# Compressed interaction network on one core: c and q chunks in blocks for unit 0, then in pairs; the stores of D split over two queues; SP waits for all gathers ahead of unit 1's x tiles

## The chip, the core and the metric

One core of a Trainium2 chip runs the whole program. The metric is the device time of one launch in microseconds (us), lower is better. The kernel before takes 185.9 us (median of 3 runs, 185.22 to 186.16).

## The reference

The input x has 512 samples, 40 features and 16 embedding columns d. Three layers are chained; each forms all products of a feature of x with a feature of the layer before and contracts them with a weight:

```python
for Wk, bk in zip(Ws, bs):
    z = jnp.einsum('bid,bjd->bdij', base, curr)
    curr = jnp.einsum('bdij,ijh->bhd', z, Wk) + bk[None, :, None]
    logit.append(curr)
pooled = jnp.sum(jnp.concatenate(logit, axis=1), axis=-1)
out = pooled @ lin_w + lin_b
```

W0 is 40 x 40 x 100, W1 and W2 are 40 x 100 x 100. Only the sum over d and the product with lin_w are wanted of the second and third layer, so the kernel folds W2 with lin_w into small vectors v, and v with W1 into one matrix D over pairs of features. What is left per sample and d is: c1 = (x x) times W0, q = (x x) times D (both 101 rows, the extra one carries the biases), and the sum of c1 * q over rows and d.

## The kernel before, in words

**The products.** A column of work is one sample and one d. 16 d times 512 samples are cut into U = 8 units of N = 1024 columns. The symmetric pairs of 41 features (the 41st is a constant one) are laid on K = 126 partitions in C = 7 chunks per unit, so there are NCH = 56 chunks, numbered m; unit 0 is m = 0 to 6, unit 1 is m = 7 to 13. The product tile of chunk m is formed by VectorE (`form`, L246), rounded by ScalarE to fp32r (`round_high`, L324, z_high) and its rest is taken by VectorE (`split`, L253, z_low). z_high and z_low have SLOTS = 14 places. In unit 0 the second factor comes from six small selection matmuls (`select_xb`, L476), later from a load of the tile xb_z (`load_xb`, L171) beside one x tile per unit (`load_xa`, L168), both by SP's DMA queue.

**The matmuls.** `chunk_products` (L434) is 6 matmuls: (high weight, high z), (low weight, high z), (high weight, low z), each for two halves of 512 columns. It is called by `c1_chunk` with W0's weights wc and by `q_chunk` with D's weights wq. The trace writes buffers without numbers: c_ps is the bank of c1, q_ps that of q. c1 of a unit is copied out by ScalarE (`copy_c1`, L331), q times c1 is added up by VectorE (`product`, L261 and L263). TensorE runs c1 LAG = 8 chunks ahead of q: c1 of m = 0 to 7 alone, then q(m), c1(m + 8) in turn, then the last eight q alone. The last two q chunks are done half by half (`last_q`, L443), and a short tail of VectorE, TensorE and ScalarE ends the program.

**The weights of q.** v comes from 40 small matmuls over W2 (`v_piece`, L495), a turn (L504) and a copy (`v_sb`, L356). D is made in NG = 5 groups (`d_group`, L518 and L521): each holds 5 lower features on partitions 0 to 63 and 5 upper ones on 64 to 127; group 4 holds the last lower feature alone. Two PSUM halves alternate, ScalarE copies each to SBUF (`copy_d`, L338, tile w_d), and a store (`store_d`, L159) writes it to d_dram: six stores on SP's queue, one on POOL's. When all have landed, 12 gathers (`gather_d`, L153) read it back in another layout into pair_sb. A gather has a side (0: contiguous rows of 808 or 2020 bytes; 1: rows of 404 bytes), one of T = 3 thirds of the partitions, and a piece: piece 0 is for chunks 0 and 1, piece 1 for chunks 2 to 6. ScalarE issues side 1 of piece 0, SP the other nine. Then the two sides are added, rounded and split: for chunks 0 and 1 by VectorE (`first_weights`, L279 to L284), for chunks 2 and 3 and then 4 to 6 by POOL (L419, L422, L424).

**The order.** All is written by hand, one stream per engine, with semaphores between. SP's stream is: x tile and first xb tile, W0's first part, small constants, the rest of W0, W2 (4 loads), W1 (4 loads), then unit 1's x tile (L195), unit 1's xb tiles for chunks 0 and 1, the stores, xb 2, three gathers, xb 3, six gathers, xb 4 to 6.

## Time and profile before

| | us |
|---|---|
| median of 3 runs | 185.9 (185.22 to 186.16) |
| profiled execution, its own time | 186.29 |
| its span, first to last instruction | 184.5 |
| TensorE busy in the span | 175.8 (95%) |
| VectorE busy | 151.8 (82%) |
| ScalarE busy | 73.9 (40%) |
| POOL busy | 16.2 (9%) |

The span is what the views show; launch and end around it are the other 1.8 us. All times in the rows count from the start of the span. A row of the timeline gives start, duration, engine, line, operation, tile written and tiles read, how many instructions were merged, and in brackets the idle time before it and what ended it. Consecutive matmuls overlap in the rows, so the distance between starts is what one costs, not its duration. Granted clock is 1.000 over the whole span.

### The profile page before, as it was taken

Reading aid. Unit: us, or ns where it says so; the run is one execution under the profiler, and the core shown is the slowest. Engines: PE = TensorE matmul, PEld = TensorE weight load, DVE = VectorE, ACT = ScalarE, POOL = GpSimd, SP = SyncE. Lnnn points to the kernel's source line nnn. Section 1 sums busy time; section 2 is a strip of 40 time slices with the busy share of each in tenths; the row PEclk is TensorE's granted clock in tenths of the full one; section 3 lists DMA queues with packets and bytes.
Section 4 is the critical chain, followed back from the end, with each engine's and each line's share of the span. In section 5 each row is a group of like instructions: output and inputs, shape, how many; then the busy total and the mean of one; then the engine's idle time right before and its main releaser. Section 6 shows DMA issues by size and latency. Waiting matters only on the chain.

```text
span 184.5 us, 2573 instructions
## 1 busy us (share of the span) xinstructions
PE 175.8 (95%) x814; PEld 118.7 (64%) x814; DVE 151.8 (82%) x135; ACT 73.9 (40%) x79; POOL 16.2 (9%) x21
## 2 busy tenths in 40 slices
PE   7798998869999999999999999999999999999994
PEld 2364474546677777777777777777777777777760
DVE  0699698869999999999999999999999999300622
ACT  2554664124444624462446244534453445002001
POOL 3670010087000000000000000000000000000000
PEclk9999999999999999999999999999999999999999
DMA  6999997999797739774986597659765200000000
GB/s 192 379 409 411 412 219 218 231 406 397 230 324 233 234 122 321 247 227 124 331 230 228 126 322 235 223 135 329 228 219 128 99 0 0 0 0 4 0 0 0
DMA packets 11845, 37.71 MB, mean 204 GB/s; under 512 B 2305, under 2 KB 2941, under 8 KB 11838
## 3 DMA queue, kind: packets, MB, share of 16 engines
q1 hardware_dynamic: 11538, 37.38, 62.1%
q0 software_dynamic: 48, 0.16, 0.3%
q10 hardware_dynamic: 252, 0.09, 0.3%
q8 instruction: 4, 0.07, 0.2%
q14 instruction: 3, 0.02, 0.0%
HBM read 36.28 MB, written 1.33 MB: 204 GB/s over the span
## 4 chain that ended last, share of the span: by engine, by line
PE 79%; DMA 8%; SPq 3%; POOL 3%; issue 2%; DVE 1%; ACT 1%; DVEq 0%; ACTq 0%
PE q_ps L434 39%; PE c_ps L434 36%; DMA pair_sb<-d_dram 3%; DMA pair_sb<-w_pairs 3%; DMA d_dram<-w_d 2%; PE q_ps L518 2%; SPq L153 2%; POOL pair_sb L401 1%; POOL wq_low L424 1%; PE q_ps L443 1%; POOL wc_low L406 1%; DVE xb_z L246 1%; ACT z_high L324 1%; SPq L159 1%; PE c_ps L565 1%
## 5 line engine op out<-in xcount | busy, mean ns | idle before, releaser
L324 ACT ACTIVATE z_high<-xb_z 126x1024 fp32r<-126x1024 f32 x56 | 59.2, 1060 | 73.0 <-DVE xb_z L246 69.3
L253 DVE TENSOR_TENSOR z_low<-xb_z,z_high 126x1024 fp32r<-126x1024 f32 x56 | 68.9, 1232 | 1.1 <-ACT z_high L324 0.8
L246 DVE TENSOR_TENSOR xb_z<-x_a,xb_z 126x1024 f32<-126x1024 f32 x50 | 62.1, 1242 | 8.3 <-DMA xb_z<-xw 8.3
L434 PE MATMUL q_ps<-z_high,wq_high 126*101 126x512 f32 x108 | 34.1, 396 | 3.0 <-POOL wq_low L424 1.5
L434 PE MATMUL c_ps<-z_high,wc_high 126*101 126x512 f32 x112 | 35.5, 398 | 0.2 <-issue 0.2
L434 PE MATMUL c_ps<-z_high,wc_low 126*101 126x512 f32 x112 | 35.0, 394 | 0.0
L434 PE MATMUL c_ps<-z_low,wc_high 126*101 126x512 f32 x112 | 35.0, 394 | 0.0
L434 PE MATMUL q_ps<-z_high,wq_low 126*101 126x512 f32 x108 | 33.8, 394 | 0.0
L434 PE MATMUL q_ps<-z_low,wq_high 126*101 126x512 f32 x108 | 33.7, 393 | 0.0
L434 PEld LDWEIGHTS q_ps<-z_high,wq_high 126*101 126x101 f32 x108 | 17.7, 165 | 10.8 <-POOL wq_low L424 2.0
L434 PEld LDWEIGHTS c_ps<-z_high,wc_high 126*101 126x101 f32 x112 | 18.0, 165 | 9.0 <-issue 1.6
L434 PEld LDWEIGHTS c_ps<-z_high,wc_low 126*101 126x101 f32 x112 | 18.5, 165 | 7.5
L434 PEld LDWEIGHTS c_ps<-z_low,wc_high 126*101 126x101 f32 x112 | 18.5, 165 | 7.4
L434 PEld LDWEIGHTS q_ps<-z_high,wq_low 126*101 126x101 f32 x108 | 17.9, 166 | 7.3
L434 PEld LDWEIGHTS q_ps<-z_low,wq_high 126*101 126x101 f32 x108 | 17.8, 165 | 7.2
L261 DVE TENSOR_TENSOR w_post<-q_ps,w_post 101x1024 f32<-101x1024 f32 x7 | 8.5, 1216 | 12.0 <-PE q_ps L434 12.0
L331 ACT ACTIVATE w_post<-c_ps 101x1024 f32<-101x1024 f32 x8 | 8.1, 1010 | 14.1 <-PE c_ps L434 14.1
L263 DVE TENSOR_TENSOR acc<-acc,w_post 101x1024 f32<-101x1024 f32 x7 | 8.6, 1226 | 0.2
L485 PE MATMUL q_ps<-warm_sb 128*128 128x512 bf16 x20 | 6.2, 483 | 1.4 <-POOL warm_sb L393 1.4
L267 DVE TENSOR_TENSOR w_post<-q_ps,w_post 101x256 f32<-101x256 f32 (+1 forms) x3 | 1.4, 508 | 5.2 <-PE q_ps L443 5.2
L388 ACT ACTIVATE out_sb<-c_ps,const_sb 1x512 f32<-1x512 f32 x1 | 0.7, 678 | 12.2 <-PE c_ps L568 12.2
L485 PEld LDWEIGHTS q_ps<-warm_sb 128*128 128x128 bf16 x20 | 2.3, 121 | 4.7 <-issue 2.2
(56 smaller groups left out, 66.1 us busy)
## 6 DMA issues: line engine op xcount, KB each, us to landing
xb_z<-xw SPq DMA_DIRECT2D x50, 512.0 KB, 4.5
x_a<-xa SPq DMA_DIRECT2D x8, 512.0 KB, 5.0
w_d<-w2h SPq DMA_DIRECT2D x4, 512.0 KB, 7.4
w_post<-w1x SPq DMA_DIRECT2D x3, 512.0 KB, 10.0
...
```

What stands on the lines that cost most here:

```text
L153: eng.dma_start(q_sides[P * t:P * (t + 1), side, c0 * J:c1 * J].rearrange("p (c j) -> p c j", j=J), src).then_inc(dpair_loaded[piece], 16)
L159: eng.dma_start(d_dram[r0:r1, column * J:(column + n) * J], w2_d[DR * upper + r0:DR * upper + r1, first * J:(first + n) * J]).then_inc(sto ...
L246: nc.vector.tensor_tensor(xb_z[0:K, c, :], x_a[0:K, u % 2, :], x_b, ALU.mult).then_inc(z_done, 1)
L253: nc.vector.tensor_tensor(z_low[0:K, m % SLOTS, :], xb_z[0:K, c, :], z_high[0:K, m % SLOTS, :].bitcast(fp32), ALU.subtract).then_inc(low_d ...
L261: nc.vector.tensor_tensor(prod, q_ps[u % 2][0:J, :], c1_sb[u % 2], ALU.mult).then_inc(q_psum_free, 1)
L263: nc.vector.tensor_tensor(acc[:, :], acc[:, :], prod, ALU.add).then_inc(acc_done, 1)
L324: nc.scalar.activation(z_high[0:K, m % SLOTS, :], xb_z[0:K, m % C, :], ACT.Copy).then_inc(high_done, 1)
L331: nc.scalar.activation(c1_sb[u % 2], c1_ps[u % 2][0:J, :], ACT.Copy).then_inc(c1_copied, 1)
L401: nc.gpsimd.tensor_tensor(side[:, :, 0, :], side[:, :, 0, :], side[:, :, 1, :], ALU.add).then_inc(wc_sums, 1)
L434: last = nc.tensor.matmul(ps[0:J, h * B:(h + 1) * B], w[0:K, c * J:(c + 1) * J], z[0:K, slot, h * B:(h + 1) * B], start=(c == 0 and k == 0 ...
L485: nc.tensor.matmul(warm_ps, warm_sb[:, 0:128], warm_sb[:, :], start=True, stop=True)
L518: last = nc.tensor.matmul(d_ps[g % 2][0:DR, 0:n], v_sb[:, :], w1_post[0:J, first:first + n], start=True, stop=True)
```

## The change

Seven things are changed.

1. **TensorE's order** (LAG is gone). After the D groups: c1 of m = 1 to 6, then q of m = 0 to 6, then c1(m), q(m) in turn, and c1(54), c1(55) ahead of the last q.
2. **The D groups** run in the order 4, 0, 1, 2, 3, with W1's loads in that order; c1(1) no longer stands between them. VectorE copies groups 1 and 3 (`copy_d` in its own stream), ScalarE 4, 0 and 2.
3. **Upper features** are placed by UPPER_AT, so that the group of features 31 to 35 and 36 to 40 is stored first, and the wrapped columns at the left of d_dram come from groups 0, 1 and 2.
4. **Stores**: seven on SP's queue, three on ScalarE's (upper half), none on POOL's; DS = 10 of them are awaited.
5. **Gathers**: SP issues all of side 0, ScalarE all of side 1.
6. **Unit 1's tiles**: SP waits until both pieces of the gathers have landed, then loads the x tile and the seven xb tiles of unit 1. W0's last part (chunks 3 to 6) is loaded after W1; its rounding on ScalarE stands after the stores.
7. **Weights of q**: VectorE prepares chunks 0 and 1 and chunks 2 and 3, POOL only 4 to 6. The product of unit u stands at m = 16 + 7u in VectorE's stream instead of 20 + 7u, the copy of c1 at 13 + 7u in ScalarE's instead of 16 + 7u.

```diff
-LAG = 8
 BODY = 2 * C
-PRODUCT_AT = 20
-C1_AT = 3 * C - LAG
+PRODUCT_AT = 16
+C1_AT = 2 * C - 1
...
-W1_CUTS = (0, 1, 2, 3, NG)
+W1_CUTS = (0, 1, 2, 3, 4, NG)
+W1_ORDER = (4, 0, 1, 2, 3)
+D_ORDER = (4, 0, 1, 2, 3)
+UPPER_AT = (31, 36, 26, 21)
...
-DS = 6
+DS = 10
...
-PREP_AT = 9
-GATHER_AT = 8
+GATHER_AT = 7
...
-            for i in range(1, len(WC_CUTS) - 1):
-                load_w0(i)
+            load_w0(1)
             for i in range(VP):
                 load_w2(i)
-            for i in range(len(W1_CUTS) - 1):
+            for i in W1_ORDER:
                 load_w1(i)
-            load_xa(1, 1)
-            for c in range(2):
-                sp.wait_ge(low_done, c + 1)
-                load_xb(1, c)
+            load_w0(2)
+            sp.wait_ge(dgroup_copied, 1)
+            store_d(sp, 0, LEFT + 4 * GI, 4 * GI, LOWER - 4 * GI, (0, DR))
             sp.wait_ge(dgroup_copied, 2)
-            store_d(sp, 0, LEFT, 0, 2 * GI, d_stored)
-            store_d(sp, 1, LEFT + LOWER, 0, 2 * GI, d_stored)
-            store_d(sp, 0, LEFT + F, 0, RIGHT, d_stored, (32, DR))
-            sp.wait_ge(dgroup_copied, 4)
-            store_d(sp, 0, LEFT + 2 * GI, 2 * GI, 2 * GI, d_stored)
-            store_d(sp, 1, LEFT + LOWER + 2 * GI, 2 * GI, 2 * GI, d_stored)
-            sp.wait_ge(dgroup_copied, NG)
-            store_d(sp, 0, LEFT + 4 * GI, 4 * GI, LOWER - 4 * GI, d_stored)
-            sp.wait_ge(low_done, 3)
-            load_xb(1, 2)
+            sp.wait_ge(dgroup_copied_dve, 1)
+            store_d(sp, 0, LEFT, 0, 2 * GI, (0, DR))
+            store_d(sp, 0, LEFT + F, 0, RIGHT, (32, DR))
+            sp.wait_ge(dgroup_copied, 3)
+            store_d(sp, 0, LEFT + 2 * GI, 2 * GI, GI, (0, DR))
+            store_d(sp, 1, LEFT - 2 * GI, 0, 2 * GI, (0, 32))
+            store_d(sp, 1, 0, 3 * GI - (LEFT - 2 * GI), LEFT - 2 * GI, (0, 32))
+            sp.wait_ge(dgroup_copied_dve, 2)
+            store_d(sp, 0, LEFT + 3 * GI, 3 * GI, GI, (0, DR))
             sp.wait_ge(equals_cleared, 1)
             sp.wait_ge(d_stored, 16 * DS)
-            sp.wait_ge(d_stored_pool, 16)
             for side, t, piece in GATHER:
-                if piece == 1 and (side, t) == (0, 0):
-                    sp.wait_ge(low_done, 4)
-                    load_xb(1, 3)
-                if side == 0 or piece > 0:
+                if side == 0:
                     gather_d(sp, side, t, piece)
-            for c in range(4, C):
+            for piece in range(len(WQ_CUTS) - 1):
+                sp.wait_ge(dpair_loaded[piece], 16 * sum(g[2] == piece for g in GATHER))
+            load_xa(1, 1)
+            for c in range(C):
                 sp.wait_ge(low_done, c + 1)
                 load_xb(1, c)
...
+            def copy_d(g):
+                dve.wait_ge(dgroup_done, D_ORDER.index(g) + 1)
+                nc.vector.tensor_copy(w2_d[:, g * GI * J:(g + 1) * GI * J], d_ps[0]).then_inc(dgroup_copied_dve, 1)
...
                 for m in range(m0, m0 + BODY):
+                    if m == 5:
+                        copy_d(1)
+                    if m == C:
+                        split(it, C - 1)
+                        first_weights(0)
+                        first_weights(1)
                     form(it, m)
+                    if m == 5:
+                        copy_d(3)
                     if m == 0:
                         split_x()
                         split(it, 0)
                     if m >= PRODUCT_AT and (m - PRODUCT_AT) % C == 0:
                         product(it, (m - PRODUCT_AT) // C)
-                    if m == PREP_AT:
-                        first_weights()
-                    if m > 1:
+                    if m > 1 and m != C:
...
+            copy_d(4)
             copy_d(0)
-            copy_d(1)
             round_high(0, 4)
             copy_d(2)
-            copy_d(3)
-            copy_d(4)
-            act.wait_ge(dgroup_copied, NG)
+            act.wait_ge(dgroup_copied, 3)
+            act.wait_ge(dgroup_copied_dve, 1)
+            store_d(act, 1, LEFT + UPPER_AT[0], 0, 2 * GI, (0, DR))
+            store_d(act, 1, LEFT + UPPER_AT[2], 2 * GI, GI, (0, DR))
+            act.wait_ge(dgroup_copied_dve, 2)
+            store_d(act, 1, LEFT + UPPER_AT[3], 3 * GI, GI, (0, DR))
+            cast_w0(2)
+            act.wait_ge(dgroup_copied, 3)
+            act.wait_ge(dgroup_copied_dve, 2)
             for m in range(5, BODY):
                 if m == GATHER_AT:
                     act.wait_ge(equals_cleared, 1)
                     act.wait_ge(d_stored, 16 * DS)
-                    act.wait_ge(d_stored_pool, 16)
-                    for t in range(T):
-                        gather_d(act, 1, t, 0)
+                    for side, t, piece in GATHER:
+                        if side == 1:
+                            gather_d(act, side, t, piece)
...
+            sum_w0(0)
+            sum_w0(1)
+            low_w0(0)
+            low_w0(1)
+            sum_w0(2)
+            low_w0(2)
             pool.wait_ge(wc_ready, len(WC_CUTS) - 1)
             nc.gpsimd.memset(q_sides[0:P, 1, 0:J], 0.0).then_inc(equals_cleared, 1)
             pool.wait_ge(equals_cleared, 1)
-            pool.wait_ge(dgroup_copied, 4)
-            store_d(pool, 1, 0, UPPER - LEFT, LEFT, d_stored_pool, (0, 32))
-            for i in range(1, len(PREP_CUTS) - 1):
-                cols = slice(PREP_CUTS[i] * J, PREP_CUTS[i + 1] * J)
-                if PREP_CUTS[i] in WQ_CUTS:
-                    piece = WQ_CUTS.index(PREP_CUTS[i])
-                    pool.wait_ge(dpair_loaded[piece], 16 * sum(g[2] == piece for g in GATHER))
-                    pool.wait_ge(wq_ready, 1)
-                nc.gpsimd.tensor_tensor(q_sides[0:K, 0, cols], q_sides[0:K, 0, cols], q_sides[0:K, 1, cols],
-                                        ALU.add).then_inc(wq_sums, 1)
-                pool.wait_ge(wq_sums, i + 1)
-                nc.gpsimd.tensor_copy(wq_high[0:K, cols], q_sides[0:K, 0, cols]).then_inc(wq_highs, 1)
-                pool.wait_ge(wq_highs, i + 1)
-                nc.gpsimd.tensor_tensor(wq_low[0:K, cols], q_sides[0:K, 0, cols], wq_high[0:K, cols].bitcast(fp32),
-                                        ALU.subtract).then_inc(wq_ready, 1)
+            cols = slice(PREP_CUTS[2] * J, PREP_CUTS[3] * J)
+            pool.wait_ge(dpair_loaded[1], 16 * sum(g[2] == 1 for g in GATHER))
+            nc.gpsimd.tensor_tensor(q_sides[0:K, 0, cols], q_sides[0:K, 0, cols], q_sides[0:K, 1, cols],
+                                    ALU.add).then_inc(last_sums, 1)
+            pool.wait_ge(last_sums, 1)
+            nc.gpsimd.tensor_copy(wq_high[0:K, cols], q_sides[0:K, 0, cols]).then_inc(last_highs, 1)
+            pool.wait_ge(last_highs, 1)
+            nc.gpsimd.tensor_tensor(wq_low[0:K, cols], q_sides[0:K, 0, cols], wq_high[0:K, cols].bitcast(fp32),
+                                    ALU.subtract).then_inc(last_ready, 1)
...
+                place = D_ORDER.index(g)
+                d_bank = d_ps[place % 2]
+                if place == 0:
                     pe.wait_ge(v_copied, 1)
-                if g == 1:
+                if place == 1:
                     pe.wait_ge(const_copied, 1)
-                if g in W1_CUTS:
-                    pe.wait_ge(w1_loaded[W1_CUTS.index(g)], 16)
-                if g >= 2:
-                    pe.wait_ge(dgroup_copied, g - 1)
+                pe.wait_ge(w1_loaded[g], 16)
+                if place == 2:
+                    pe.wait_ge(dgroup_copied, 1)
+                if place == 3:
+                    pe.wait_ge(dgroup_copied, 2)
+                if place == 4:
+                    pe.wait_ge(dgroup_copied_dve, 1)
...
+            d_group(4)
             d_group(0)
             d_group(1)
-            c1_chunk(0, 1)
             d_group(2)
             d_group(3)
             select_xb(6)
-            d_group(4)
-            for m in range(2, LAG):
+            for m in range(1, C):
                 c1_chunk(0, m)
-            whole = (NCH - LAG) // BODY
-            with pe.Fori(0, whole) as it:
-                for m in range(LAG, LAG + BODY):
-                    q_chunk(it, m - LAG)
+            for m in range(C):
+                q_chunk(0, m)
+            for m in range(C, BODY):
+                c1_chunk(0, m)
+                q_chunk(0, m)
+            with pe.Fori(0, NCH // BODY - 2) as it:
+                for m in range(BODY, 2 * BODY):
                     c1_chunk(it, m)
-            for m in range(LAG + whole * BODY, NCH):
-                q_chunk(0, m - LAG)
+                    q_chunk(it, m)
+            for m in range(NCH - BODY, NCH - 2):
                 c1_chunk(0, m)
-            for m in range(NCH - LAG, NCH - 2):
                 q_chunk(0, m)
+            for m in range(NCH - 2, NCH):
+                c1_chunk(0, m)
...
-        groups = [np.arange(g * GI, min((g + 1) * GI, LOWER)), np.arange(LOWER + g * GI, min(LOWER + (g + 1) * GI, F))]
-        part = w1f[:, np.concatenate(groups)].reshape(128, -1)
+        groups = [np.arange(g * GI, min((g + 1) * GI, LOWER)), np.arange(UPPER_AT[g], UPPER_AT[g] + GI) if g < NG - 1 else []]
+        part = w1f[:, np.concatenate(groups).astype(int)].reshape(128, -1)
```

SP's queue from W1's loads to unit 1's tiles. DMA names give the tile written and read; w0_pairs is W0, d_dram <- w2_d a store of D, pair_sb <- d_dram a gather. Before:

```order
L183 DMA w1_post<-w1x 128x1125
L168 DMA x_a<-xa 128x1024
L171 DMA xb_z<-xw 128x1024 [waits low_done] x2
L159 DMA d_dram<-w2_d 64x1010 [waits dgroup_copied]
...
L159 DMA d_dram<-w2_d 64x101 [waits dgroup_copied]
L171 DMA xb_z<-xw 128x1024 [waits low_done]
L153 DMA pair_sb<-d_dram 42x202 [waits d_stored_pool,d_stored,equals_cleared]
...
L171 DMA xb_z<-xw 128x1024 [waits low_done]
L153 DMA pair_sb<-d_dram 42x505
```

The same place of the changed kernel:

```order
L178 DMA pair_sb<-w0_pairs 128x808
L162 DMA d_dram<-w2_d 64x101 [waits dgroup_copied]
L162 DMA d_dram<-w2_d 64x1010 [waits dgroup_copied_dve,dgroup_copied]
L162 DMA d_dram<-w2_d 32x909
L162 DMA d_dram<-w2_d 64x505 [waits dgroup_copied]
L162 DMA d_dram<-w2_d 32x1010
L162 DMA d_dram<-w2_d 32x202
L162 DMA d_dram<-w2_d 64x505 [waits dgroup_copied_dve]
L156 DMA pair_sb<-d_dram 42x202 [waits d_stored,equals_cleared]
...
L156 DMA pair_sb<-d_dram 42x505 x3
L171 DMA x_a<-xa 128x1024 [waits dpair_loaded1,dpair_loaded0]
L174 DMA xb_z<-xw 128x1024 [waits low_done] x7
```

No x tile stands ahead of the stores or between the gathers any more; the first one stands behind a wait for both pieces.

VectorE's stream from the last selected product of unit 0 to unit 1's first products; xb_z is `form`, z_low is `split`, L279 to L284 are the weights of q. Before:

```order
L246 TENSOR_TENSOR xb_z<-x_a,q_ps0 126x1024 [waits selected,xa_loaded0]
L253 TENSOR_TENSOR z_low<-xb_z,z_high 126x1024 [waits z_slots_free,high_done]
L246 TENSOR_TENSOR xb_z<-x_a,xb_z 126x1024 [waits xb_loaded0,xa_loaded1]
...
L246 TENSOR_TENSOR xb_z<-x_a,xb_z 126x1024 [waits xb_loaded2,xa_loaded1]
L279 TENSOR_TENSOR pair_sb<-pair_sb 126x202 [waits dpair_loaded0]
```

The changed kernel, with the two copies of D ahead of it:

```order
L276 COPY w2_d<-q_ps1 128x505 [waits dgroup_done]
L245 TENSOR_TENSOR xb_z<-x_a,c1_ps1 126x1024 [waits selected,xa_loaded0]
L276 COPY w2_d<-q_ps1 128x505 [waits dgroup_done]
L252 TENSOR_TENSOR z_low<-xb_z,z_high 126x1024 [waits z_slots_free,high_done]
L245 TENSOR_TENSOR xb_z<-x_a,q_ps0 126x1024 [waits selected,xa_loaded0]
L252 TENSOR_TENSOR z_low<-xb_z,z_high 126x1024 [waits z_slots_free,high_done] x2
L282 TENSOR_TENSOR pair_sb<-pair_sb 126x202 [waits dpair_loaded0]
...
L282 TENSOR_TENSOR pair_sb<-pair_sb 126x202 [waits dpair_loaded1]
...
L245 TENSOR_TENSOR xb_z<-x_a,xb_z 126x1024 [waits xb_loaded0,xa_loaded1]
```

Unit 1's first product, which stood ahead of the first weights, stands behind both sets of weights.

ScalarE's stream from the rounding of z(3) to the gathers; w2_d <- q_ps1 is a copy of D. Before:

```order
L338 ACTIVATE w2_d<-q_ps1 64x101 [waits dgroup_done]
L324 ACTIVATE z_high<-xb_z 126x1024 [waits z_slots_free,z_done,dgroup_copied]
L324 ACTIVATE z_high<-xb_z 126x1024 [waits z_slots_free,z_done]
L324 ACTIVATE z_high<-xb_z 126x1024 [waits z_done,z_slots_free]
L153 DMA pair_sb<-d_dram 42x101 [waits d_stored_pool,d_stored,equals_cleared]
L153 DMA pair_sb<-d_dram 42x2x101 x2
```

The changed kernel:

```order
L347 ACTIVATE w2_d<-q_ps1 128x505 [waits dgroup_done]
L162 DMA d_dram<-w2_d 64x1010 [waits dgroup_copied_dve,dgroup_copied]
L162 DMA d_dram<-w2_d 64x505
L162 DMA d_dram<-w2_d 64x505 [waits dgroup_copied_dve]
L352 ACTIVATE wc_high<-pair_sb 126x404 [waits wc_sums]
L333 ACTIVATE z_high<-xb_z 126x1024 [waits z_done,z_slots_free,dgroup_copied_dve,dgroup_copied]
L333 ACTIVATE z_high<-xb_z 126x1024 [waits z_slots_free,z_done]
L156 DMA pair_sb<-d_dram 42x101 [waits d_stored,equals_cleared]
L156 DMA pair_sb<-d_dram 42x2x101 x2
L156 DMA pair_sb<-d_dram 42x5x101 x3
```

Three stores, the rounding of W0's last part and three more gathers have come into it.

## Rows read from the trace of the kernel before

**Rows 1.** Windows: stretch, length, busy time (instructions) of the engines, clock, DMA share, GB/s.
```profile
60.00:80.00 20.00, 20.00 (x88) 14.23 (x87) 19.96 (x19) 9.99 (x10) 0.00 (x0) 1.00 0.74 232
```

**Rows 2.** Timeline of TensorE.
```profile
16.43 0.64 PE L518 MATMUL q_ps<-w_post,v_sb 101*64 101x505 f32 x1 [0.37 <-ACT v_sb L356]
...
17.32 0.59 PE L518 MATMUL q_ps<-w_post,v_sb 101*64 101x505 f32 x1
...
21.65 0.73 PE L476 MATMUL q_ps<-z_high,select_r 126*128 126x512 f32 x2
...
22.63 0.70 PE L434 MATMUL c_ps<-z_high,wc_high 126*101 126x512 f32 x2
...
33.10 0.70 PE L434 MATMUL q_ps<-z_high,wq_high 126*101 126x512 f32 x2 [1.50 <-DVE wq_low L284]
...
40.44 0.71 PE L434 MATMUL q_ps<-z_high,wq_high 126*101 126x512 f32 x2 [1.50 <-POOL wq_low L424]
...
43.30 0.62 PE L434 MATMUL q_ps<-z_high,wq_high 126*101 126x512 f32 x2
```

**Rows 3.** Timeline of VectorE.
```profile
6.08 1.23 DVE L246 TENSOR_TENSOR xb_z<-x_a,xb_z 126x1024 f32<-126x1024 f32 x1 [6.08 <-DMA xb_z<-xw]
...
17.48 1.23 DVE L253 TENSOR_TENSOR z_low<-xb_z,z_high 126x1024 fp32r<-126x1024 f32 x1
...
31.88 0.37 DVE L279 TENSOR_TENSOR pair_sb<-pair_sb 126x202 f32<-126x202 f32 x1 [0.87 <-DMA pair_sb<-d_dram]
...
47.47 1.21 DVE L246 TENSOR_TENSOR xb_z<-x_a,xb_z 126x1024 f32<-126x1024 f32 x1
...
49.74 1.21 DVE L246 TENSOR_TENSOR xb_z<-x_a,xb_z 126x1024 f32<-126x1024 f32 x1
...
178.83 0.69 DVE L267 TENSOR_TENSOR w_post<-q_ps,w_post 101x512 f32<-101x512 f32 x1 [5.20 <-PE q_ps L443]
```

**Rows 4.** Chain of waits: start, length, what.
```profile
23.51 4.53 DMA d_dram<-w_d
...
31.58 0.41 SPq L153
...
32.04 5.49 DMA pair_sb<-d_dram
```

**Rows 5.** Timeline of ScalarE (ACTq is its DMA queue).
```profile
16.41 1.04 ACT L324 ACTIVATE z_high<-xb_z 126x1024 fp32r<-126x1024 f32 x1
17.54 0.59 ACT L338 ACTIVATE w_d<-q_ps 128x505 f32<-128x505 f32 x1
...
22.74 0.25 ACT L338 ACTIVATE w_d<-q_ps 64x101 f32<-64x101 f32 x1 [0.38 <-PE q_ps L518]
...
28.11 1.40 ACTq L153 DMA_DIRECT2D pair_sb<-d_dram  x3
```

**Rows 6.** Timeline of SP's queue.
```profile
0.76 0.41 SPq L168 DMA_DIRECT2D x_a<-xa  x1
...
19.01 5.15 SPq L159 DMA_DIRECT2D d_dram<-w_d  x6
```

**Rows 7.** Tile d_dram, all its stores.
```profile
DMA to landing us min/median/max: 3.5/4.4/4.8
```

**Rows 8.** Windows while the stores, then the gathers of piece 1 are under way.
```profile
22.00:23.00 1.00, 1.00 (x6) 0.50 (x5) 0.51 (x1) 0.61 (x2) 0.05 (x1) 1.00 1.03 409
23.00:28.00 5.00, 5.00 (x23) 3.58 (x22) 4.60 (x5) 3.07 (x3) 0.61 (x1) 1.00 0.92 232
...
34.00:36.00 2.00, 2.00 (x11) 1.36 (x10) 1.31 (x3) 0.00 (x0) 0.00 (x0) 1.00 1.15 203
```

**Rows 9.** Timeline of POOL.
```profile
37.61 0.61 POOL L419 TENSOR_TENSOR pair_sb<-pair_sb 126x202 f32<-126x202 f32 x1 [14.00 <-DMA pair_sb<-d_dram]
...
40.35 1.82 POOL L419 TENSOR_TENSOR pair_sb<-pair_sb 126x303 f32<-126x303 f32 x1
...
43.64 1.69 POOL L424 TENSOR_TENSOR wq_low<-pair_sb,wq_high 126x303 fp32r<-126x303 f32 x1
```

More of the change, by code:

```diff
@@ L154, in gather_d, with store_d @@
                          ).then_inc(dpair_loaded[piece], 16)
-        def store_d(eng, upper, column, first, n, stored, rows=(0, DR)):
+        def store_d(eng, upper, column, first, n, rows):
             r0, r1 = rows
             eng.dma_start(d_dram[r0:r1, column * J:(column + n) * J],
-                         w2_d[DR * upper + r0:DR * upper + r1, first * J:(first + n) * J]).then_inc(stored, 16)
+                         w2_d[DR * upper + r0:DR * upper + r1, first * J:(first + n) * J]).then_inc(d_stored, 16)
         def chunks(tile, c0, c1):
@@ L345, in _ @@
             nc.scalar.activation(select_r[:, :], select_sb, ACT.Copy).then_inc(select_rounded, 1)
-            for i in range(len(WC_CUTS) - 1):
-                act.wait_ge(wc_sums, i + 1)
-                nc.scalar.activation(chunks(wc_high, WC_CUTS[i], WC_CUTS[i + 1]),
-                                     w0_sides[0:K, WC_CUTS[i]:WC_CUTS[i + 1], 0, :], ACT.Copy).then_inc(wc_highs, 1)
+            cast_w0(0)
+            cast_w0(1)
             round_high(0, 1)
```

52 lines of the change are left out of this document (29 added, 23 removed).

## The prediction

> **What bounds the kernel now.** I read the windows of the steady stage first. TensorE and VectorE are both busy for all of it [rows 1], so the reader must ask which of them waits for the other. VectorE's starts tell: two instructions lie 2.27 us apart (47.47 to 49.74) [rows 3], so a chunk (form and split) costs 2.27 us and a unit 7 x 2.27 + 2.27 for its two product instructions = 18.2 us. TensorE needs 2.86 us for a pair of chunks (40.44 to 43.30) [rows 2], 2.79 us on the mean of the long stretch below. That is 19.5 us a unit. TensorE is the bound and VectorE catches up 1.3 us a unit.
>
> Then the timeline of TensorE, from the back. VectorE's last product starts at 178.83, released by the first half of the last q [rows 3]. Before it TensorE is never idle back to 40.44, where it had waited 1.50 us for POOL's weights, and it had waited 1.50 us at 33.10 for VectorE's [rows 2]. At 43.30 q(3) begins; by then c1 of m = 0 to 10 and q of 0 to 2 are done, 14 chunks. From there to the first half of the last q are 97 chunks (51 q, 45 c1, and two half chunks): (178.8 - 43.3) / 97 = 1.40 us each. The tail behind it is the same in both kernels. So the end is set by one number: when TensorE, having 14 chunks done, goes on without a gap. Before it is 43.30.
>
> The chain of waits says what made that late: the last store starts at 23.51 and lands 4.53 us later, at 28.04; the gathers follow, the last issued at 31.58 and landed at 37.53 [rows 4]; then POOL's three operations to 40.4 [rows 9].
>
> **The change: the mark to compute.** After the change 14 chunks are done when q(6) ends (c1 0 to 6, q 0 to 6), and c1(7) comes next. From there it is again 49 c1 + 47 q + 1 = 97 chunks. Call its start T; the time changes by T - 43.30. c1(7) needs TensorE free from q(6), and z(7), whose x tiles are now loaded behind all gathers. Two paths, worked out from S, the moment all stores have landed.
>
> **Copies and stores: S.** TensorE starts the first D group at 16.43 and a whole group takes 0.89 us (16.43 to 17.32) [rows 2]. Group 4 (a fifth of the columns of one half) is done by 16.7, group 0 by 17.5. ScalarE rounds z(3) until 17.45 [rows 5], then copies group 4 (0.25 us) and group 0 (0.59 us) until 18.3. Group 1 can start at 17.7 and is done at 18.7. VectorE's split(3) ends at 18.7 too [rows 3], so its copy of group 1 runs to 19.3. A VectorE copy of 505 columns from PSUM isn't in the trace; 0.59 us (ScalarE, same tile) and 0.69 us (VectorE, 512 columns, two inputs) [rows 3, 5] bound it, I take 0.6. Group 2 is done at 19.5 and copied by 20.2 behind the rounding of z(4); group 3 at 20.4, and VectorE has formed z(5) meanwhile, so its copy ends at 21.1. Before, the last copy ended at 22.99 [rows 5]. SP's seven stores: the first tiny one at 18.3, two at 19.4, three from 20.2, the last from about 22.1 (six issues took 5.15 us with their waits, so 0.5 to 0.6 each [rows 6]). ScalarE's three fall between 20.3 and 21.9. The last store starts 1.4 us earlier than 23.51. Landing takes 3.5 to 4.8 us [rows 7], measured while loads of x tiles were in the same queue; these are now gone, so I take 3.9 (between the least and the median of 4.4): S = 26.0 instead of 28.04. With 3.5 us and 4.8 us it is 25.6 and 26.9.
>
> What limits it from the other side is the rate. 1.33 MB are written, and while the stores were under way 232 GB/s flowed at a DMA share of 0.92 [rows 8], against 409 GB/s while loads and stores were mixed just before [rows 8]. If that rate also held here, the first large store would land at 19.4 + 3.5 = 22.9 and the other 1.07 MB need 4.6 us more: S = 27.5. If lower and upper half, now in two queues, go side by side at more than 232 GB/s, S is bounded by the last issue: 22.1 + 3.5 = 25.6, or 25.3 if its start is a little earlier.
>
> The Trainium skill speaks against the second queue: "DMA: Bandwidth & Descriptors", section Rules for kernel authors, says that two transfers to disjoint partition halves serialize and that spreading DMAs over SP and ScalarE only saves issue time. "SBUF — State Buffer", section Door 1, says that partitions 0 to 63 reach only half of the ports. The 232 GB/s agree with half of the ports for each store by itself; by the first page S stays at about 27.5, by the second one interleaving could lift the rate and give 25.3.
>
> **From S to q(0).** The third gather of piece 0 on ScalarE starts 1.0 us after the first (three took 1.40 us [rows 5]), piece 0 was there at 31.88, 3.8 us after 28.06 [rows 3], and TensorE started at 33.10. I keep that with a small discount for the x tile that no longer shares the engines: q(0) at S + 4.9 = 30.9. Is TensorE free? c1(1) starts after select(6), which now follows group 3: 20.4 + 0.7 = 21.1, against 22.63 for c1(2) before [rows 2]; six chunks of 1.40 us end at 29.5. W0's last part is cast on ScalarE behind the stores, at 22.4, and subtracted by POOL, 404 columns, until 23.5 to 24.5; c1(3) wants it at 23.9. So c1(6) ends between 29.5 and 30.1, and TensorE idles about 1 us instead of 1.50. All of ScalarE's six gathers are issued by S + 2.9, ahead of q(0), which waits for a signal behind them. q(0) to q(6) take 7 x 1.40 = 9.8 us: q(6) ends at S + 14.7.
>
> **Piece 1 and unit 1's tiles.** Six gathers on each queue, 0.47 us each: the last issue ends at S + 2.9. From the end of the last issue to VectorE's first weights piece 0 took 31.88 - 29.51 = 2.4 us [rows 3, 5]; piece 1 took 5.49 us [rows 4], with an xb tile ahead of it and three behind. I take 3.5, nearer to the lower because no xb tile is left: L = S + 6.4 = 32.4; the ends are S + 5.3 and S + 8.4. VectorE then needs 1.1 us for chunks 2 and 3: ready at S + 7.6, wanted for q(2) at S + 7.7. POOL's chunks 4 to 6 took 40.35 to 45.33 beside a busy VectorE [rows 9]; its sum over 202 columns, with VectorE idle, took 0.61 us, over 303 columns beside VectorE 1.82 us. VectorE is idle now for most of that time, so 3.6 us: S + 10.1, wanted at S + 10.5. If it took the 4.98 us, 1 us more of idle.
>
> SP issues the x tile at L + 0.1. In the prologue x tile and xb tile were issued from 0.76 on and VectorE started at 6.08 [rows 3, 6], 5.3 us; with the engines already warm and idle, I take 4.9 (4.3 to 5.3). form(7) at L + 5.0; form(8) waits for the next 0.5 MB, 1.3 us; then split(7): z(7) is complete 3.7 us after form(7) starts, T = L + 8.7 = 41.1. The TensorE path gives S + 14.7 = 40.7. The later one counts: T = 41.1, a gain of 2.2 us.
>
> **What the tiles' delay costs later.** form(7), which stood ahead of the first weights (31.88), moves to 37.4. From then on VectorE gains 2.79 - 2.27 = 0.52 us a chunk on TensorE and pays 2.27 us for each product, the first at m = 16: c1(15) finds z(15) 1.9 us early, c1(22) 3.3 us early. Seven xb tiles stand in the queue at once at 1.3 us each, faster than 2.27. So no new stall. At the end c1(55) now comes just ahead of the last q; its copy (1024 columns on ScalarE, as the 1.04 us of a rounding [rows 5]) lies beside the first half of last q (1.40 us). Nothing.
>
> **Sum.** The profiled execution took 186.29; 186.29 - 2.2 = 184.1. It is 0.4 above the median of 185.9, so I say 185.9 - 2.2 = 183.7 for the likeliest case.
>
> **Rivals.**
> - *The halves go side by side* (S = 25.3, L = S + 5.2 = 30.5). TensorE's path decides: T = 40.0 and gain 3.3, time 182.6. For it: the low rate of single stores at a nearly full share. Against: the gathers' own packets are slow, 203 GB/s at a share of 1.15 [rows 8]. Chance 0.18.
> - *The stores keep their rate* (S = 27.5, L = 33.9): T = 42.6, gain 0.7, time 185.2. For it: the rows of the store stage, and the Trainium skill's rule above. Then the second queue does not do what it is there for. Chance 0.19.
> - *Slower: unit 1's tiles become the bound.* Place: VectorE's form(7). Price: T = L + 8.7, and before no product waited for the gathers. The point is L = 34.6; later than that the kernel loses. Piece 1 took 9.5 us from S before (28.04 to 37.53). If it keeps that with S = 26.0, L = 35.5, T = 44.2: 0.9 us lost, 186.8. Against: an xb tile of 0.5 MB stood ahead of it and its nine gathers on SP were issued one after the other until 32.0 [rows 4]. Chance 0.10.
> - *The wait at q(0) grows* over 2 us, and TensorE's clock falls to 1.2 GHz, where a chunk would cost twice 1.40 us. The two waits of 1.50 us [rows 2] left a chunk at its 1.40 us and the clock at 1.00 [rows 8]. Chance 0.03, about 186.5.
>
> The likeliest case has 0.50, its own range is 182.9 to 184.7. What a measurement of this kernel can tell from no change is about 0.5%, 0.93 us. Faster than 184.97: nearly all of the likeliest, the first rival and a third of the second, 0.74. Within: 0.16. Slower than 186.8: 0.10. The range that should hold 8 in 10 is 182.3 to 186.2.
>
> **What would show it.** In the changed profile: the last store issued near 22.1 and landed near 26.0; q(0) at 30.9 after about 1 us of idle; no wait of TensorE within q(0) to q(6); form(7) at 37.4 after some 4 us in which VectorE waited for xb; c1(7) at 41.1, at most 0.5 us after q(6); from there no gap, and the same 135.5 us from c1(7) to the start of the last product. It is wrong if the stores land after 27, if piece 1 lands more than 7 us after them, if POOL's three operations hold up q(4), or if a later c1 waits for a split.

## The result, and the profile after the change

The changed kernel takes 183.63 us (median of 5 runs, 183.48 to 184.47) against 185.9 for the kernel before in the same comparison: ratio 0.9876, 95% interval 0.984 to 0.9913. Forecast were 183.7 us and "faster". The profiled execution is the slowest of the five, 184.47 with a span of 182.7; before it was 186.29, so the profile has 1.8 of the 2.3 us. Runs over 1.5% above the fastest of their kernel count as slow, and medians and ratios here leave them out (five of `e9`'s twelve, one of `e11`'s six).

The page of the changed kernel:

```profile
span 182.7 us, 2555 instructions
...
PE 175.1 (96%) x814; PEld 118.8 (65%) x814; DVE 152.8 (84%) x140; ACT 72.7 (40%) x77; POOL 9.8 (5%) x17
```

TensorE's timeline: its last wait at q(0), and c1(7), the mark of the prediction. These answer to [rows 2]:

```profile
31.95 0.71 PE L453 MATMUL q_ps<-z_high,wq_high 126*101 126x512 f32 x2 [1.39 <-DVE wq_low L287]
...
41.82 0.63 PE L453 MATMUL c_ps<-z_high,wc_high 126*101 126x512 f32 x2
```

VectorE's, answering to [rows 3] (the copies of D's groups 1 and 3, the weights of both pieces, form(7), the last product):

```profile
18.48 0.68 DVE L276 COPY w_d<-q_ps 128x505 f32<-128x505 f32 x1
...
21.00 0.68 DVE L276 COPY w_d<-q_ps 128x505 f32<-128x505 f32 x1 [0.72 <-PE q_ps L547]
...
30.82 0.37 DVE L282 TENSOR_TENSOR pair_sb<-pair_sb 126x202 f32<-126x202 f32 x1 [3.82 <-DMA pair_sb<-d_dram]
...
32.59 0.37 DVE L282 TENSOR_TENSOR pair_sb<-pair_sb 126x202 f32<-126x202 f32 x1 [0.70 <-DMA pair_sb<-d_dram]
...
37.55 2.54 DVE L245 TENSOR_TENSOR xb_z<-x_a,xb_z 126x1024 f32<-126x1024 f32 x2 [3.17 <-DMA xb_z<-xw]
...
177.02 0.69 DVE L266 TENSOR_TENSOR w_post<-q_ps,w_post 101x512 f32<-101x512 f32 x1 [9.85 <-PE q_ps L462]
```

The last product starts at 177.02 instead of 178.83: this is the whole difference. It is 135.2 us behind c1(7), against 135.5 behind the mark before, so 1.5 of the 1.8 us were gained by the mark and 0.3 behind it. What matters lies ahead of 41.82. There the stores land at 26.34 (28.04 before) by the chain of waits, which answers to [rows 4] (start, length, what):

```profile
22.17 0.89 SPq L162
23.06 0.04 issue
23.10 3.23 DMA d_dram<-w_d
...
27.46 3.33 DMA pair_sb<-d_dram
...
31.95 10.04 PE q_ps L453 x42
```

and piece 1 lands at 32.59 instead of 37.53, 6.25 us behind the stores instead of 9.5. POOL's share of the last weights, [rows 9] before, is done by 35.1:

```profile
32.71 0.94 POOL L438 TENSOR_TENSOR pair_sb<-pair_sb 126x303 f32<-126x303 f32 x1 [7.76 <-DMA pair_sb<-d_dram]
33.72 0.44 POOL L441 CAST wq_high<-pair_sb 126x303 fp32r<-126x303 f32 x1
34.23 0.84 POOL L443 TENSOR_TENSOR wq_low<-pair_sb,wq_high 126x303 fp32r<-126x303 f32 x1
```

### The profile page after: what moved, and what is told of

Same layout as the page of the kernel before. It is cut to its first block, busy times and chain, and to the rows that moved or that the text cites. A ratio compares the mean times of both kernels' runs of the same rounds, so it can differ in the third digit from the quotient of the medians.

```text
span 182.7 us, 2555 instructions
## 1 busy us (share of the span) xinstructions
PE 175.1 (96%) x814; PEld 118.8 (65%) x814; DVE 152.8 (84%) x140; ACT 72.7 (40%) x77; POOL 9.8 (5%) x17
## 3 DMA queue, kind: packets, MB, share of 16 engines
HBM read 36.28 MB, written 1.33 MB: 206 GB/s over the span
## 4 chain that ended last, share of the span: by engine, by line
PE 86%; DMA 6%; DVE 2%; SPq 2%; issue 1%; ACTq 1%; ACT 0%; DVEq 0%
PE q_ps L453 41%; PE c_ps L453 38%; DMA xb_z<-xw 2%; SPq L162 2%; DMA pair_sb<-d_dram 2%; DMA d_dram<-w_d 2%; PE q_ps L516 1%; PE c_ps L497 1%; PE q_ps L544 1%; PE q_ps L462 1%; DVE z_high L271 1%; PE q_ps L497 1%; PE c_ps L594 1%; ACTq L156 1%; PE c_ps L597 0%
## 5 line engine op out<-in xcount | busy, mean ns | idle before, releaser
L245 DVE TENSOR_TENSOR xb_z<-x_a,xb_z 126x1024 f32<-126x1024 f32 x50 | 60.9, 1218 | 9.6 <-DMA xb_z<-xw 9.5
L544 PE MATMUL q_ps<-w_post,v_sb 101*64 101x505 f32 (+1 forms) x10 | 4.4, 537 | 0.8 <-ACT v_sb L368 0.4
```

The source lines that it names most:

```text
L245: nc.vector.tensor_tensor(xb_z[0:K, c, :], x_a[0:K, u % 2, :], x_b, ALU.mult).then_inc(z_done, 1)
L544: last = nc.tensor.matmul(d_bank[0:DR, 0:n], v_sb[:, :], w1_post[0:J, first:first + n], start=True, stop=True)
```

## The experiments

The marks are those of the prediction: S all stores landed, L piece 1 landed. All ratios are to the kernel before, run beside each kernel. "A" and "B" are the theories of each quoted text.

Every run has its granted clock, averaged over its span, beside its time. Runs of one kernel fall into two groups by it: most have 0.998 to 1.000, some 0.991 and less. The kernel before is in the lower group in 18 of its 69 runs beside the experiments, with a median of 186.8 us against 185.7. `e12` shows such a fall in its trace. Where a kernel has both groups, both are given.

**The stores by themselves** (`e7_store_rates`). A kernel of stores alone. In four stages it writes lower halves on SP; lower and upper by turns on SP; lower on SP and upper on ScalarE; whole tiles of 128 partitions.

> Only stores, nothing of the function is computed. Four stages, each 2.07 MB, each after the one before has landed: (1) eight stores of 64 lower partitions x 1010 columns on SP; (2) eight on SP, lower and upper by turns; (3) four lower on SP and four upper on ScalarE at the same time; (4) four stores of 128 partitions on SP. Theory A (a store of 64 partitions alone is limited by its half of the ports): (1) near 220 GB/s, (2) and (3) above it, (4) near 400. Theory B (the rate is that of writing to memory, or halves serialize): all of (1) to (3) near 230 GB/s; then (4) tells the two apart, 230 or 400.

One window of each stage (the last three numbers are granted clock, DMA share, GB/s):

```profile
14.00:15.00 1.00, 0.00 (x0) 1.00 1.01 206
24.00:25.00 1.00, 0.00 (x0) 1.00 0.91 307
35.00:36.00 1.00, 0.00 (x0) 1.00 0.98 372
42.00:43.00 1.00, 0.00 (x0) 1.00 1.03 412
```

Apart from the windows in which a stage begins (202 in the second, 109 and 190 in the third) or ends, the stages had 194 to 210, 247 to 307, 299 to 372 and 396 to 416 GB/s. That is what A expected: halves do go side by side, also from one queue, more so from two. That two transfers to disjoint partition halves serialize, as the Trainium skill's "DMA: Bandwidth & Descriptors" has it in its section Rules for kernel authors, does not hold for these stores of 64 partitions to HBM. That partitions 0 to 63 reach half of the ports, as the Trainium skill's "SBUF — State Buffer" has it in its section Door 1, fits the first row, which has half the rate of the last.

**The D part alone** (`e9_stores_gathers_only`): the kernel before with the new order of D's groups and columns, the copies on two engines, W0's last part late, ten stores and split gathers. Unit 1's tiles, the weights and TensorE's order stay old. Its core:

```diff
+D_ORDER = (4, 0, 1, 2, 3)
-DS = 6
+DS = 10
...
-                if side == 0 or piece > 0:
+                if side == 0:
```

> The kernel before with only what is ahead of the weights changed: order of the D groups, copies on two engines, ten stores on two queues, side 1 of all gathers on ScalarE, W0's last part late. TensorE's order, the places of unit 1's tiles and the weights (VectorE chunks 0 and 1, POOL 2 to 6) are those of before. Theory A (the gain is earlier stores and gathers; the block order and the wait only suit each other): stores land near 27, piece 1 near 35 with tiles beside it, q(2) at about 37.3 instead of 40.44, both waits of 1.5 us gone or nearly, 182.9 us (182.4 to 184). Theory B (order and wait are needed): piece 1 at 37 or later, 185 us or more.

186.45 us, ratio 1.0014 (0.9973 to 1.0054): nothing gained, A is wrong. SP's queue, POOL's wait, TensorE's wait at q(2) and the clock there:

```profile
17.12 7.34 SPq L163 DMA_DIRECT2D d_dram<-w_d  x7
...
28.16 1.17 SPq L157 DMA_DIRECT2D pair_sb<-d_dram  x3
```

```profile
37.59 0.62 POOL L444 TENSOR_TENSOR pair_sb<-pair_sb 126x202 f32<-126x202 f32 x1 [12.95 <-DMA pair_sb<-d_dram]
```

```profile
41.17 0.70 PE L459 MATMUL q_ps<-z_high,wq_high 126*101 126x512 f32 x2 [2.49 <-POOL wq_low L449]
```

```profile
41.00:42.00 1.00, 0.83 (x4) 0.64 (x5) 1.00 (x1) 0.00 (x0) 1.00 (x2) 1.00 1.06 422
```

The stores leave nearly as early as in the changed kernel (17.12 + 7.34 = 24.5 against 24.07) and still land at 28.1; piece 1 lands 9.4 us later. Both are the numbers of the kernel before. The DMA engines still moved 372 to 412 GB/s from 20 to 25, loads and stores mixed, where the changed kernel's moved 157 to 271. After the wait of 2.49 us the clock stayed at 1.00.

**All but the D part** (`e12_old_d_part`): the kernel before, with the change's TensorE order, late tiles, weights on two engines and split gathers:

```diff
-PRODUCT_AT = 20
-C1_AT = 3 * C - LAG
+PRODUCT_AT = 16
+C1_AT = 2 * C - 1
-            load_xa(1, 1)
-            for c in range(2):
-                sp.wait_ge(low_done, c + 1)
-                load_xb(1, c)
...
+            for piece in range(len(WQ_CUTS) - 1):
+                sp.wait_ge(dpair_loaded[piece], 16 * sum(g[2] == piece for g in GATHER))
+            load_xa(1, 1)
```

> The changed kernel with the D part of before: groups 0 to 4 in order, all copies on ScalarE, six stores on SP and one on POOL, W0's last part early. Late tiles, split gathers, block order and weights stay as changed. Theory A (the tiles' new place, not the D part, moved the stores' landing): the last store is issued at 23.5 as before, with no tile in the queue it lands 3 to 3.5 us later, at 26.5 to 27.0 instead of 28.04; c1(7) starts at about 41.5, 183.6 to 184.4 us. Theory B (the D part carries the earlier landing): it lands at 28, c1(7) at 43, 185.3 us or more.

186.16 us, ratio 0.9988 (0.9953 to 1.0023): again nothing, the time that B named and not my A's. By the clock the twelve runs are four at full clock, 185.10 to 185.38 us, and eight at 0.991, 185.88 to 186.98. The profile is of the second kind. SP's queue, TensorE's wait and the windows behind it:

```profile
19.14 5.19 SPq L159 DMA_DIRECT2D d_dram<-w_d  x6
27.85 2.48 SPq L153 DMA_DIRECT2D pair_sb<-d_dram  x6
```

```profile
32.44 1.18 PE L427 MATMUL q_ps<-z_high,wq_high 126*101 126x512 f32 x2 [2.46 <-DVE wq_low L278]
```

```profile
32.00:33.00 1.00, 0.56 (x2) 0.43 (x3) 0.37 (x1) 0.00 (x0) 0.00 (x0) 0.57 0.69 137
33.00:34.00 1.00, 1.00 (x4) 0.72 (x3) 0.13 (x1) 0.00 (x0) 0.07 (x1) 0.50 0.00 0
...
36.00:37.00 1.00, 1.00 (x6) 0.71 (x5) 0.00 (x0) 0.00 (x0) 0.35 (x1) 1.00 1.00 401
```

The copies keep the last store until 23.69; it lands 4.09 us later, S = 27.8, though no tile stands in the queue. The gathers gain (L = S + 6.1), but TensorE now waits 2.46 us at q(0), its clock falls to 0.50 (1.2 GHz) towards the end of that wait, and it is at 1.00 again from 36 on. q(0) to q(6) take 11.2 us instead of 9.87 (from q(0) to c1(7): 32.44 to 43.66, and 31.95 to 41.82). So all but the D part is worth 0.5 to 0.7 us while the clock stays up (185.2 against 185.7 to 185.9 for the kernel before at full clock), and the fall takes that back in two runs of three. With the D part S comes 1.5 us earlier, and none of the changed kernel's five runs has the lower clock. Two variants of it, `e1` and `e5`, have it in four runs of twelve and three of nine.

**TensorE's order alone** (`e4_order_only`), put on the kernel before:

```diff
-PRODUCT_AT = 20
-C1_AT = 3 * C - LAG
+PRODUCT_AT = 16
+C1_AT = 2 * C - 1
-            for m in range(2, LAG):
+            for m in range(2, C):
```

> The kernel before with only TensorE's new order (c1 0 to 6, q 0 to 6, then c1(m), q(m) in turn; products at m = 16 + 7u, copies of c1 at 13 + 7u). Theory A (the order alone loses, since without the c1 chunks between them q(2) and q(4) wait for POOL's weights of 40.4 and 45.3): q(4) at 45.4, q(6) ends at 49.6, 14 chunks done 6.3 us later than 43.30, 192 us. Theory B (the order is what gains): 184 us.

191.79 us, ratio 1.0285 (1.0233 to 1.0337), as A had it. Two waits, and the clock behind them:

```profile
32.40 0.71 PE L434 MATMUL q_ps<-z_high,wq_high 126*101 126x512 f32 x2 [2.33 <-DVE wq_low L284]
...
40.03 1.18 PE L434 MATMUL q_ps<-z_high,wq_high 126*101 126x512 f32 x2 [3.05 <-POOL wq_low L424]
...
44.95 0.71 PE L434 MATMUL q_ps<-z_high,wq_high 126*101 126x512 f32 x2 [0.43 <-POOL wq_low L424]
```

```profile
34.00:35.00 1.00, 1.00 (x4) 0.60 (x3) 0.95 (x1) 0.00 (x0) 0.00 (x0) 0.50 1.26 232
...
42.00:43.00 1.00, 1.00 (x4) 0.72 (x3) 1.00 (x2) 0.14 (x1) 1.00 (x1) 0.50 1.03 410
```

**The old order in the changed kernel** (`e10_old_order`), the reverse of that edit:

> The changed kernel with TensorE's order of before (c1 0 to 7 alone, then q(m), c1(m + 8)), products and copies at their old places. Theory A (the late tiles need the block): c1(7) must wait for z(7) at 41.2, q(0) starts at 42.6 with 8 chunks done instead of 14, 9 us later than now, 192.8 us, more if the clock falls in the long wait (12 us idle). Theory B (the order is of little weight): under 187 us.

195.19 us, ratio 1.0495 (1.0446 to 1.0543), the direction of A and 2.4 us above its number. c1(7) stands ahead of the first q chunks and waits for the late tile:

```profile
41.45 1.15 PE L454 MATMUL c_ps<-z_high,wc_high 126*101 126x512 f32 x2 [11.12 <-ACT z_high L334]
```

Its clock falls to 0.50 within that wait and stays there until nearly 45. So the late tiles need the order of blocks (without it 11.6 us more than the changed kernel, the clock's part included), and the blocks need piece 1 of the weights early (6 us, `e4`).

**Tiles not held back** (`e2_tiles_unbound`):

```diff
-            for piece in range(len(WQ_CUTS) - 1):
-                sp.wait_ge(dpair_loaded[piece], 16 * sum(g[2] == piece for g in GATHER))
```

> The changed kernel without SP's wait for the gathers ahead of unit 1's x tiles; the tiles follow the last gather in SP's queue. Theory A (TensorE's path through q(0) binds, the tiles only just do not): z(7) is ready near 37 instead of 41.2, piece 1 lands at most 0.7 us later, c1(7) still follows q(6) at 41.8, 183.6 us, within 0.4. Theory B (the wait protects the gathers from 4 MB of tiles on the same engines): piece 1 lands 2 us or more later than 32.6, q(2) or q(4) waits for its weights, 185 us or more.

186.3 us, ratio 1.0056 (1.0015 to 1.0096): B, though piece 1 lands 1.8 us later than in the changed kernel and not 2. Taking the wait out loses the whole gain. By the clock the ten runs are six at full clock, median 186.0, and four at 0.991, near 188.0.

```profile
34.40 0.37 DVE L280 TENSOR_TENSOR pair_sb<-pair_sb 126x202 f32<-126x202 f32 x1 [2.71 <-DMA pair_sb<-d_dram]
```

```profile
36.22 0.71 PE L451 MATMUL q_ps<-z_high,wq_high 126*101 126x512 f32 x2 [1.44 <-DVE wq_low L285]
```

Piece 1 comes at S + 8.1 and q(2) waits. Until piece 1 landed the tiles flowed beside it, up to 348 GB/s in all from 33 to 34. That ScalarE's gathers were late because they shared the engines with them is argued from this; the next run bears on it.

**No wait, but all gathers of piece 1 in SP's queue ahead of the tiles** (`e11_piece1_one_queue`):

```diff
-                if side == 0:
+                if side == 0 or piece > 0:
...
-            for piece in range(len(WQ_CUTS) - 1):
-                sp.wait_ge(dpair_loaded[piece], 16 * sum(g[2] == piece for g in GATHER))
```

> As the kernel without the wait (tiles unbound, 186.3 us), but all six gathers of piece 1 stand on SP's queue ahead of the tiles; ScalarE issues only side 1 of piece 0. Theory A (the 404-byte packets on ScalarE's ring lost their turns to the 4096-byte packets of the tiles on SP's): in one ring they come first; piece 1 lands near 33, 184 us. Theory B (tiles hold up gathers in either ring): piece 1 at 34.4 or later, 186 us or more.

184.15 us, ratio 0.9898 (0.9853 to 0.9942): A. A sixth run took 218.5 us at a mean granted clock of 0.759; why the clock was low is open. SP's queue and VectorE:

```profile
26.13 3.79 SPq L156 DMA_DIRECT2D pair_sb<-d_dram  x9
29.97 0.40 SPq L171 DMA_DIRECT2D x_a<-xa  x1
```

```profile
32.44 0.37 DVE L280 TENSOR_TENSOR pair_sb<-pair_sb 126x202 f32<-126x202 f32 x1 [1.59 <-DMA pair_sb<-d_dram]
...
35.38 2.50 DVE L243 TENSOR_TENSOR xb_z<-x_a,xb_z 126x1024 f32<-126x1024 f32 x2 [1.16 <-DMA xb_z<-xw]
```

The tiles start 2.5 us before L here and do little harm: they are behind the gathers in one queue, not beside them in another. They also start 1.1 us later than in `e2` (29.97 against 28.86), and how much of the difference is that and how much the queue is not separated. Also form(7) comes 2.2 us earlier and the time doesn't fall: VectorE's tile did not set c1(7).

**One queue for the stores** (`e1_one_queue`): ScalarE's three stores are issued by SP.

> The changed kernel with all ten stores of D on SP's queue (ScalarE issues none). Theory A (the end of the stores is set by when the last one is issued): nine large stores from 19.25 at some 0.5 us each put the last issue at about 24.0 instead of 23.10, the stores land at 27.3 instead of 26.34, c1(7) starts 1 us later, 184.6 us. Theory B (the bytes set it, halves serialize): landing stays at 26.3, 183.6 us. Theory C (lower and upper half side by side from two queues raise the rate): landing 1.5 to 2 us later, 185.4 us.

184.29 us, ratio 0.9939 (0.9905 to 0.9972). The last store starts at 24.00 and lands 2.37 us later, S = 26.37, unchanged, as B had it; ten issues end at 24.6:

```profile
17.04 7.56 SPq L162 DMA_DIRECT2D d_dram<-w_d  x10
```

The runs fall in two groups, eight near 184.1 at full clock and four near 185.8 at 0.991. At full clock it is 0.5 us above the changed kernel, which is not settled.

**All copies of D on ScalarE** (`e5_copies_scalar`):

> The changed kernel with all five copies of D on ScalarE. Theory A (the copies on VectorE save one wait for the rounding of z): group 3 is copied at about 22 as now (it waits for W1's load until 19.9), the last store moves by under 0.4 us, 183.6 to 184.0 us. Theory B (two copying engines carried the earlier stores): last store 1 us later, 184.6 us.

184.23 us, 0.9926 (0.9892 to 0.996). It overlaps with the changed kernel's interval. The medians differ by 0.6 us, by 0.4 for the six runs at full clock: VectorE's part in the copies is worth little here. The last store on the way to S starts at 22.06, 1.04 us earlier than in the changed kernel, and lands 4.47 us later, S = 26.55.

**Chunks 2 and 3 of the weights on POOL instead of VectorE** (`e3_pool_weights`):

> The changed kernel with the weights of chunks 2 and 3 prepared by POOL again, ahead of 4 to 6; VectorE only prepares chunks 0 and 1. Theory A (POOL is quick while VectorE waits): chunks 2 and 3 ready at about 34.4, wanted at 34.8; 4 to 6 ready at 36.8, wanted at 37.6; nothing moves, 183.6 us. Theory B (moving them to VectorE carried part of the gain): they take the 2.8 us of before, q(2) starts 0.6 us late and q(4) up to 2 us late, 184.2 to 186 us.

183.84 us, 0.9886 (0.9855 to 0.9917): A, no difference. POOL has chunks 2 and 3 ready at 33.92, 1.74 us after it began; q(2) starts at 33.97, under 0.2 us late. In the changed kernel VectorE takes 1.79 us for them (32.59 to 34.38), with POOL at work beside it: its cast takes 0.79 us instead of the 0.27 alone, its subtraction 0.56 instead of 0.37.

**Unit 1's x tile and first xb tile ahead of the stores** (`e8_tile_early`):

```diff
+            load_xa(1, 1)
+            sp.wait_ge(low_done, 1)
+            load_xb(1, 0)
```

> The changed kernel with unit 1's x tile and its first xb tile loaded ahead of the stores, behind W0's last part. Theory A: 1 MB more in the queue from 18 to 20.5, when the engines were nearly idle; the stores land up to 1 us later and the whole is 0 to 1 us slower than the changed kernel, since z(7) did not bind. Theory B (VectorE's wait for the tiles binds): c1(7) earlier, 183 us or less.

184.0 us, 0.9896 (0.9857 to 0.9936): A. S = 26.31; two tiles of 0.5 MB ahead of the stores do no harm and no good. They flow from 18 to 21 (397, 418 and 322 GB/s), before most bytes of the stores. `e9` has a third tile ahead of the stores and one right behind them, and there S is 28.1.

**A block of eight** (`e6_block_of_eight`): on top of that edit, c1(7) stands in the block ahead of q(0), where TensorE waits.

```diff
-            for m in range(1, C):
+            for m in range(1, C + 1):
...
-                c1_chunk(0, m)
+                if m > C:
+                    c1_chunk(0, m)
```

> As the kernel with the early tile, and c1(7) in TensorE's block ahead of q(0), where TensorE waits 1.4 us in the changed kernel. Theory A: one chunk more is done when q(6) ends, so 1.4 us are gained, less what the stores land later (0 to 1 us): 182.2 to 183.2 us, unless z(8), whose xb tile now comes first behind the gathers, is late at q(7). Theory B (what lands later eats it): 183.6 us or more.

VectorE's first weights and ScalarE's gathers move one chunk later with it. 182.51 us (182.34 to 182.87), ratio 0.9812 (0.9775 to 0.9849): A, faster than both kernels, each of its six runs below each of the changed kernel's, and 1.5 us below `e8`, from which it differs by the block alone. Without idling TensorE goes from c1(7) to q(0):

```profile
30.99 0.63 PE L455 MATMUL c_ps<-z_low,wc_high 126*101 126x512 f32 x2
31.46 0.62 PE L455 MATMUL q_ps<-z_high,wq_high 126*101 126x512 f32 x2
```

## Why the prediction was right

The size was right, forecast 183.7, measured 183.63, and so was the mechanism from S on. How S comes about was not: the number of that step is luck. Step by step, in the profiled execution:

| step | forecast | measured |
|---|---|---|
| last store issued | 22.1 | 23.10 |
| its landing | 3.9 | 3.23 |
| S | 26.0 | 26.34 |
| TensorE's idle at q(0) | about 1 | 1.39 |
| q(0) | S + 4.9 = 30.9 | S + 5.6 = 31.95 |
| q(0) to c1(7) | 9.8 | 9.87 |
| L | 32.4 | 32.59 |
| form(7) | 37.4 | 37.55 |
| c1(7) | 41.1 | 41.82 |
| c1(7) to the last product | 135.5 | 135.2 |

*S.* I took the issue of the last store plus a landing time, and was right by two errors that cancel. SP issued its stores more slowly while ScalarE issued at the same time: up to 1.15 us for one, where I took 0.5 to 0.6 (alone, in `e1`, up to 0.95). In return the last landed faster than the row of before. But S does not follow the last issue at all:

| | last store starts | lands after | S |
|---|---|---|---|
| `e5` | 22.06 | 4.47 | 26.55 |
| changed kernel | 23.10 | 3.23 | 26.34 |
| `e1`, one queue | 24.00 | 2.37 | 26.37 |

The starts are those of the issue; counted from its end (23.79, 24.07, 24.60) the landing shrinks as well. What the three have in common is the flow of bytes, here for the changed kernel, `e1` and `e5`:

```profile
20.00:26.00 6.00, 5.63 (x24) 3.29 (x25) 4.69 (x6) 2.71 (x4) 2.06 (x3) 1.00 0.84 220
...
20.00:26.00 6.00, 6.00 (x28) 4.29 (x27) 5.38 (x6) 2.56 (x3) 2.34 (x3) 1.00 0.83 218
...
20.00:26.00 6.00, 4.60 (x20) 2.70 (x17) 3.10 (x3) 3.23 (x5) 2.57 (x3) 1.00 0.91 218
```

That is the 1.33 MB of the stores, from 20 on. My other reason, that no x tile is in the queue, holds for the amount and not for the tile as such: with two tiles ahead S is 26.3 (`e8`), with three ahead and one behind 28.1 (`e9`), where loads still fill the engines. Without tiles but with the old D part S is 27.8 (`e12`), with a window of 77 GB/s at 23 while the late copies hold up the stores. So S wants the first large store out early, no gap behind it, and the loads done by then. This is read from the windows; no run changed the amount of bytes. Why the flow has 220 GB/s here and 299 to 372 in `e7`'s third stage stays open.

*The rate of the stores* (second rival, 0.19). Single windows of the changed kernel reach more than the 232 GB/s of [rows 8] (clock, share, GB/s last):

```profile
22.00:23.00 1.00, 1.00 (x6) 0.73 (x5) 1.00 (x2) 0.00 (x0) 0.00 (x0) 1.00 0.99 271
...
24.00:25.00 1.00, 0.63 (x3) 0.23 (x2) 0.41 (x2) 1.00 (x2) 0.89 (x2) 1.00 0.97 259
```

On the mean of 21 to 26 it is 232 again. So the rival's rate held and its sum was wrong: it let the bytes begin with the landing of the first large store at 22.9, and they flow from 20 on. The first rival's premise, halves side by side, holds (`e7`), yet S did not come at 25.3; `e5`, with its last issue at 22.06, did not reach it either. One queue gives the same S (`e1`), so the second queue is not where S came from. That interleaving two stores could lift the rate was my own inference from the ports, not a statement of the Trainium skill.

*q(0)* is the mis-sized term, by 0.7 us. In this execution piece 0 came at S + 4.5. In those of `e1`, `e8` and `e11`, whose stores landed at 26.37, 26.31 and 26.1, q(0) started at 30.78, 31.07 and 30.90, on my 30.9, and c1(7) at 41.07, 41.06 and 41.30, near my 41.1. They are kernels of 181.9 to 182.2 us of span, and the changed kernel's other executions had 181.7 to 181.9, against 182.7 in the profiled one. I take the profiled one as late by this, which is argued from these numbers and not shown.

*T.* I let VectorE's path decide (41.1) over TensorE's (40.7). z(7) was complete at 41.2, as said. TensorE's path ended 0.6 us behind that, at 41.8 instead of 40.7, because of q(0). `e11` agrees: with form(7) at 35.4 the time is no lower. The 0.4 between my two paths was less than the error of either.

*The weights of chunks 2 to 6.* I gave VectorE 1.1 us for chunks 2 and 3 and POOL 3.6 us for the rest, since VectorE would be idle. It was not: both began when L came. VectorE took 1.79 us and POOL 2.36 us. The two misses did not reach TensorE in the profiled execution, where q(0) was late; in `e1` and `e11` they make q(2) wait 0.23 and 0.34 us.

*The tiles' delay* costs nothing later, as forecast: no gap of TensorE follows. It also protects the gathers: L - S was forecast 6.4 and is 6.25. The bounds were 5.3 and 8.4, and `e2` lands at 8.1, near the upper one: the wait is worth 2 us, the whole gain. The third rival (tiles become the bound, 0.10) needed L = 34.6. `e2`'s L of 34.40 came close, but there q(2) waited for the weights, not c1(7) for its tile: the place I had given it was wrong.

*The clock* (0.03). The chance was too low. I judged by two waits of 1.50 us that left the clock alone. It did so after 1.39 here too, but `e12`'s fell to half with a wait of 2.46 us and `e4`'s with one of 2.33, while `e9`'s stayed up after 2.49, and `e12`'s own did in four runs of twelve. So the length of one wait does not decide it, and the kernel before has the lower clock in 18 runs of 69. Had q(0) waited 1 us more, that could have cost some 1.3 us on top (11.2 less 9.87).

*Interaction.* What I did not say is that the parts have no gain one by one: D part alone 1.00, the rest alone 1.00, order alone 1.03, all but the order 1.05, together 0.988. S gates q(0), and S and the tiles' place together gate L. Whichever is mended alone, TensorE keeps a wait of some 2.5 us: at q(0) in `e12`, for piece 1 in `e9`. And in `e12` part of the missing gain is the clock: its runs at full clock take 185.2 us.
